# The kept scores of a top-k attention: one VectorE instruction per tile in place of two on GpSimd

## The reference

```python
scores = jnp.einsum('bhqd,bhkd->bhqk', Q, K) / np.sqrt(d)
k_keep = int(s * (1.0 - SPARSITY))                 # 25 of 256
vals, idx = jax.lax.top_k(scores, k_keep)
sparse = jnp.zeros((n, s), scores.dtype).at[rows, idx].set(vals)   # the rest is 0
attn = jax.nn.softmax(sparse, axis=-1)
out = jnp.einsum('bhqk,bhkd->bhqd', attn, V)
```

## Time and profile before

| what | value |
|---|---|
| three runs | 6017.2, 6035.1, 6035.79 us; median 6035.1 |
| the profiled execution, its own time | 6033.22 us |
| its span, first to last instruction | 6031.4 us |
| busy: PE, DVE, ACT, POOL | 5402.1, 4518.6, 3706.0, 2307.4 us |
| L1044, 4096 replaces, of these x1024 with m_last | mean 423 to 424 ns |
| granted TensorE clock, mean over the span | 0.934 |

### The profile page before, as it was taken

How to read it: one execution, slowest core, us unless ns; L and a number is a source line. 1 busy time by engine, 2 the same in 40 slices (tenths; PEclk the granted TensorE clock), 3 DMA queues, 4 the chain that set the end, 5 groups by cost and what they waited for, 6 DMA issues and landing times. The chain is left out here.

```text
span 6031.4 us, 113615 instructions
## 1 busy us (share of the span) xinstructions
PE 5402.1 (90%) x39450; PEld 3816.4 (63%) x39450; DVE 4518.6 (75%) x16189; ACT 3706.0 (61%) x9249; POOL 2307.4 (38%) x4100
## 2 busy tenths in 40 slices
PE   7899999899898999899998898989999899999987
PEld 4666666666666666566666666666666666666654
DVE  2477887777887777787777887777887777887774
ACT  3466676666676666666665666656666666676542
POOL 0233443334443334443333443334443334443341
PEclk7799999999999999999999999999999999998876
DMA  2000000000000000000000000000000000000000
GB/s 88 4 5 7 8 8 6 7 8 5 8 7 10 5 8 5 9 8 8 5 8 7 7 8 8 5 7 6 8 8 6 7 8 6 7 7 8 3 5 6
DMA packets 29387, 53.44 MB, mean 9 GB/s; under 512 B 8145, under 2 KB 9810, under 8 KB 27986
## 3 DMA queue, kind: packets, MB, share of 16 engines
q1 hardware_dynamic: 28770, 45.73, 2.5%
HBM read 37.33 MB, written 8.39 MB: 8 GB/s over the span
## 5 line engine op out<-in xcount | busy, mean ns | idle before, releaser
L1044 DVE MATCH_REPLACE8 wk<-m,wk 128x256 f32<-128x256 f32 x2048 | 835.9, 423 | 0.0
L1065 POOL TENSOR_SCALAR mx<-m 128x2 f32<-128x2 f32 x512 | 114.3, 223 | 1761.2 <-DVE wk L1044 1755.9
L479 DVE TENSOR_REDUCE m_nm<-bankM 128x2 f32<-128x512 f32 x1024 | 656.4, 692 | 168.6 <-PE bankM L469 166.4
L1040 DVE MAX8 m<-wk 128x8 f32<-128x256 f32 x2048 | 772.0, 425 | 0.0
L1074 POOL TENSOR_TENSOR t_pr<-wk,sc 128x256 f32<-128x256 f32 x1024 | 738.1, 741 | 3.8 <-issue 1.4
L1077 POOL TENSOR_TENSOR t_pr<-t_pr,sc 128x256 f32<-128x256 f32 x1024 | 728.4, 732 | 0.0
L810 ACT ACTIVATE xk_area<-bankH,xb 64x256 f32<-64x256 f32 x1024 | 479.8, 469 | 296.3 <-PE bankH L712 278.1
L1001 ACT ACTIVATE t_pr<-t_pr,t_nm 128x256 f32<-128x256 f32 x1024 | 475.9, 510 | 153.8 <-POOL t_pr L1077 141.5
L528 PE MATMUL bankM<-m_q,m_kT 32*128 32x512 f32 x2048 | 565.1, 631 | 0.0
L469 PE MATMUL bankM<-m_kT,m_q 32*128 32x256 f32 x4096 | 535.6, 399 | 10.3 <-DVE m_nm L479 8.9
L570 PE MATMUL bankT<-ident,t_pr 128*128 128x128 f32 x2048 | 342.9, 292 | 120.1 <-ACT t_pr L1001 117.7
(11 more groups left out here) (223 smaller groups left out, 11926.7 us busy)
## 6 DMA issues: line engine op xcount, KB each, us to landing
xin<-x_in SPq DMA_DIRECT2D x32, 256.0 KB, 2.6
ctxA<-ctx_in SPq DMA_DIRECT2D x32, 256.0 KB, 2.6
ctxB<-ctx_in SPq DMA_DIRECT2D x32, 256.0 KB, 2.8
out<-x SPq DMA_DIRECT2D x32, 256.0 KB, 2.0
w<-w_w SPq DMA_DIRECT2D x2, 1024.0 KB
xwq<-w_xwq SPq DMA_DIRECT2D x1, 1024.0 KB
xwk<-w_xwk SPq DMA_DIRECT2D x1, 1024.0 KB
xwv<-w_xwv SPq DMA_DIRECT2D x1, 1024.0 KB
```

What stands on the lines that cost most here:

```text
L479: nc.vector.tensor_reduce(b["nm"][:, i % 2, 2 * (i // 2) + x, :], banks[u % 4][:].rearrange("p (j s) -> p j s", j=2), AX.X, ALU.max, negat ...
L1040: link.inc(nc.vector.max(top, src[:, t, :]))
L1044: m = nc.vector.match_replace(out=wk[:, k, t, :], in_to_replace=take, in_values=src[:, t, :], imm_value=-BIG)
```

## The change

The two GpSimd instructions and their semaphore `sp_tk` go. VectorE makes the kept scores with one SCALAR_TENSOR_TENSOR per tile, (wk equals -2^64) times sc, right behind the head's last replace, and now waits itself for the transposes of head u-2. The exponential loses its scale. The buffer, the shift and all that TensorE does stay.

```diff
-        taken = sp_ = bufT["pr"]
+        sp_ = bufT["pr"]
...
                     nc.scalar.activation(b["pr"][:, u % 2, t, :], sp_[:, u % 2, t, :], ACT.Exp,
-                                         bias=b["nm"][:, u, t:t + 1], scale=-1.0 / BIG).then_inc(g["spa_ex"], 1)
+                                         bias=b["nm"][:, u, t:t + 1]).then_inc(g["spa_ex"], 1)
...
                 if u >= 2:
-                    dve.wait_ge(*at(g["sp_tk"], NT * (u - 1)))
                     dve.wait_ge(*at(g["sp_nm"], u - 1))
...
                     src = wk[:, k]
+                if u >= 2:
+                    dve.wait_ge(*at(g["spa_tr"], u - 1))
+                for t in range(NT):
+                    dve.wait_ge(*at(g["sp_top"], NT * u + t + 1))
+                    nc.vector.scalar_tensor_tensor(sp_[:, k, t, :], wk[:, k, t, :], -BIG, sc[:, u % 3, t, :], ALU.is_equal, ALU.mult).then_inc(g["sp_mul"], 1)
...
                 nc.gpsimd.tensor_copy(b["nm"][:, u, :], mx0[:, u, :]).then_inc(g["spa_nm"], 1)
-                yield
-                if u >= 2:
-                    pool.wait_ge(*at(g["spa_tr"], u - 1))
-                for t in range(NT):
-                    pool.wait_ge(*at(g["sp_top"], NT * u + t + 1))
-                    nc.gpsimd.tensor_tensor(taken[:, u % 2, t, :], wk[:, u % 2, t, :], sc[:, u % 3, t, :], ALU.subtract).then_inc(g["sp_tk"], 1)
-                for t in range(NT):
-                    pool.wait_ge(*at(g["sp_tk"], NT * u + t + 1))
-                    nc.gpsimd.tensor_tensor(sp_[:, u % 2, t, :], taken[:, u % 2, t, :], sc[:, u % 3, t, :], ALU.mult).then_inc(g["sp_mul"], 1)
```

```diff
     "pool": runs("""
-        c2 t h t2 c h2 t h t6 c t2 m t9 h2 t m t2 m h t h t3 h c t c t2 c t2 h t2 h t h t4 m t3 h c h t3 m t6 h2 t c2 t3 h2 t3 h t3 c t6 h
```

More of the change, by code:

```diff
@@ L79 @@
     "pe": runs("""
[L80 to L83, removed]
@@ new lines @@
+        c2 t c m h c h2 m2 t c h t h2 t m c m h c h2 t m2 h t m t h m t m h m c m h t h2 m h2 m t m2 t m2 t m2 h m h m t m t h t h2 m t m2 h3 t
+        h t h4 m h2 m2 h c h t m t m h t m t c2 t h3 c h2 t c h3 t2 h2 t h2 c t h t h t c h t c3 t h c t h t2 h2 c t c h4 c2 t h t c t c h c t
+        c2 h t2 h2 t h c2 t h3 t c2 t c h t h c h t h c2 h c t h t h c t c t h t h t c2 h c t h2 t h8 c h c t c t c t c t c t c2 t3 c t2 c t2 c
+        t2 c t c t c t2 c2 t c5 t c t2 c3 t c2 t c t2 c t c2 t4 c3 t3 c t5 c32"""),
@@ L99 @@
-        t6 h t3 h t3 h t h t8 h3 c5 t c t20 c t12 h t9 c2 t c t8 c t2 c7"""),
+        c2 t c h t2 h2 t h m t8 c m t2 m h t8 h t2 h t2 h c3 h t3 h t h2 m t4 h2 t c t h t2 c2 h t h t h t8 h t4 h c t2 h t2 h t2 h t4 h t2 h t2
+        h t h t5 h3 c5 t c t15 c t14 c3 t6 c7"""),
 }
@@ new lines @@
+        h c m h2 t c h t c t c h2 c t m h3 t h t2 c h2 m c m2 t h m2 t h m h t m h t m h m h m h t m h m t m t m t m5 t c m2 h t m h t m3 t m h
+        m2 h t m h t m t m h4 t h4 t h c h3 c t2 h t c t c2 m t c2 h2 c h2 t h c2 h t h2 c h t h c t h c t h c h c t c h t c h c2 t c h c t c h2
+        c2 t h c3 t h3 c t h c t h c h t h c h2 t h m t c t c h2 m2 t m h m2 h2 m t m h t h m t m h2 m2 t h t m t m t m2 t m4 h m2 t m t h m3 t
+        m h m2 h t m h t m t m h6 t h2 t h"""),
+    "act": runs("""
+        h2 c h t c h c h t h c t2 h t2 c h t5 h t h2 t h3 m t h2 t2 h t h2 t h t h2 t c2 h2 c t2 h2 t c2 h t h t2 c h2 t c2 t h2 t h2 c t c2 h t
+        h3 t c3 h4 t c h t h2 c t h3 c t c h t c h2 t h3 t h t c t h4 t h t3 h m t h2 t h3 t c h t h t h3 m4 t4 h2 t2 h t h t h t h2 t4 m t m t
+        m2 t m2 t m t c m2 t4 m2 t h m3 h t3 m2 t m2 h t h t m t h t m h t h2 c h c t h t h t c t3 h t3 c h t h t h7 t3 h2 t2 h3 t2 h t h2 c t
+        h2 t c2 h t h c2 t h2 t c t c t m t h2 t c h4 t c3 h4 t2 c3 h2 t h2 c t3 h t c h5 c2 h t c h t h4 t3 h c h5 t4 h t h m h t h c h3 t m t2
+        h m h m t m t h3 t2 h t2 h3 t3 h2 t5 m t m t m t2 m4 t2 m2 t2 m2 t h m3 t h t2 m2 t m h m t h m t2 h t m h t h c h2 t h c h2 c t h t c
+        t4 h c h t4 h t h2 t h3 t h t h3 t m t h t h t h2 t c2 h t h t h2 c t c2 t h t c h t h2 t c2 t h2 t h2 c t c t c h4 t c3 h4 t2 c h c h2
+        t h3 c t c h t c h t h4 t c h t2 h4 t h t3 h m t h2 t h3 t c t h2 t h2 m4 t3 h t h2 t h t h t h t h t h t4 m t m2 t c m2 t m2 t2 m2 t4
+        m2 h t m3 h t3 m2 t m2 t h2 t m t h t m h t h2 t h c h2 t h c t c t2 h t2 c h t3 h t h6 t3 h t h4 t3 h t h c t h3 c2 t h t h c2 t h2 t3
+        c m c t h2 t c h4 t c3 h4 t c t c2 h2 t h2 c t4 c h6 c2 h t c h t h4 t h t2 c h5 t4 h t h m t c h4 t h t2 m h2 m2 t m t h t h3 t h t2 h2
+        t h t h t6 m t m t2 m t m4 t2 m2 t2 m2 t h m3 h t3 m h m t m t m h m t2 h t m h t h"""),
@@ L136 @@
+        t2 h t h c2 t h c t5 h2 t2 m t2 h2 t2 c h t4 c t2 h t m t h c h t2 h t2 c t6 h t2 h m h t2 m t2 h c t c t h t h c t3 h2 t m t c t2 h2 m
+        t6 h c2 t2 h t h t h t4 c t2 h t4 h t2 m h t2 m h t h t c3 t2 h t2 h2 t h t3 m t2 h2 t2 h t4"""),
 }
@@ L159 @@
               mla_m3=1, mla_m3p=1, mla_nm=16, mla_on=2, mla_onT=1, mla_ont=1, mla_ot=2, mla_ott=1, mla_pv=8, mla_q=1, mla_qT=2, mla_rd=2,
-              mla_s=16, mla_sp=4, mla_st=16, mla_v=1, mla_va=1, mla_x=1, mla_y=1, sp_mul=32, sp_nm=16, sp_sc=16, sp_tk=32, sp_top=32,
+              mla_s=16, mla_sp=4, mla_st=16, mla_v=1, mla_va=1, mla_x=1, mla_y=1, sp_mul=32, sp_nm=16, sp_sc=16, sp_top=32,
               sp_xb=1, spa_ex=32, spa_k=1, spa_kT=2, spa_nm=16, spa_on=2, spa_onT=1, spa_ont=1, spa_ot=8, spa_ott=1, spa_pt=16, spa_pv=8,
```

82 lines of the change are left out of this document (33 added, 49 removed).

## The result

The changed kernel takes 1.0495 times as long as the one before (95% interval 1.0455 to 1.0534), 4.95% or about 299 us more. The profiled execution took 6334.2 us with a span of 6332.4, another 6318.5; two further executions were much slower, 6477.4 us at a granted clock of 0.799 and 20205.0 us, and are left out, so the ratio rests on two executions of the changed kernel. The forecast was 6175 us with a range up to 6300: the sign was right, the size about half of what was measured, and the time lies outside the range.

What follows compares the result with a forecast made beforehand. VectorE's unbroken row up to L907, for which TensorE waits at L768, was taken as the bound. Per lap 8.1 - 2.4 - 0.65 = +5.0 us; 28 laps +141, others +2, on 6033.2 gave 6175 us, range 6060 to 6300.

Steps and rivals of the forecast that it cites:

- The price of the instruction: New VectorE pair behind each head's last replace: 0.79 us a head, taken from L898, making 8.1 us a lap.
- rival 3: Much slower: GpSimd locks out the new VectorE instruction nearly every time, +15.2 us a lap, 6458 us; chance 0.07.
- the wait for `spa_tr`: New pair's first instruction waits for TensorE's transposes of the head before last; priced at nothing, over 30 us meaning wrongly priced.
- the forecast's 840: GpSimd's busy time was to fall from 2307 to some 840 us once its subtractions and products go.
- The bound: For the 80-odd us ahead of L907 VectorE runs without pause; time added there moves L768 and all behind it.
- a forecast of 5.0: Growth of a loop lap: 8.1 added, less 2.4 from quieter GpSimd, less 0.65 idle, +5.0 us.
- 10.25 heads: Heads per lap, of 16, whose new pair lies in VectorE's full stretch ahead of L907 and so costs time.
- a longer low clock: Longer wait at L768 may lengthen TensorE's 1.2 GHz stretch behind it, 1.7 us a lap; upper bound only.
- Time added outside falls into idle time: VectorE work outside its full stretch, five or six of a lap's 16 heads, costs nothing, since VectorE waits for TensorE there.
- The wait at L768: TensorE's wait for VectorE's L907 in stream h was to rise from 4.0 to some 9 us every loop lap.
- a wait under 5 us: Sign at L768: a wait this short would mean VectorE's stretch had cover that the forecast didn't see.
- The relief: VectorE's L902, L907 and lnM_xn run faster without GpSimd's pair beside them: 2.4 us a lap, 67 us in all.

Runs made afterwards that it cites:

- the kernel without the step: Changed kernel without VectorE's new pair, ScalarE taking the exponential of all scores, so the selection is missing from the output: 5973.0 us, 0.9922 of the kernel before.
- the pair with fillers: Two kernels with one more filler everywhere: kernel before plus two MAX8 per head on VectorE, GpSimd's pair kept, 6294.7 us; changed kernel, 6239.6 us.
- the MAX8 stand-in: Kernel before, GpSimd's two instructions kept, with two unused MAX8 per head added on VectorE, old fillers: 6291.7 us, 1.0438 of the kernel before.

## Why the prediction was half right

- **The price of the instruction** was near, and somewhat high: one takes 417 ns, and the pair moves the next start by 0.67 us (2850.81 to 2851.48 in the rows below) where the sum used 0.79. L1053 itself is never locked out beside GpSimd, so rival 3 falls, and so does any cost of the wait for `spa_tr` (1.2 us over the span). What collides is held on GpSimd's side, its copy L1072. That is 198 of the 262 us by which GpSimd's 1102.7 us exceed the forecast's 840.
- **The bound** held in its place: a lap grows only ahead of L907. Its size is not confirmed. With the clock repaired at five places a lap grows by 5.3 us for a forecast of 5.0, but 266 fillers and 2.9 us of low time (worth 1.4 us) are in the 5.3, and with one more filler everywhere on both sides it grows by 4.4, 2.0 without the low clock. Inside the 5.0, too, two misses cancel: 10.25 heads at 0.67 us are 6.9 us and not 8.1, and the stretch from L898 to L907's end shrank by 1.0 us (3.55 to 2.54) and lnM_xn gave 0.3, 1.3 together and not 2.4. The agreement is partly luck.
- **The step that failed** is the clock, "a longer low clock" priced at nothing in the sum and at up to 1.7 us a lap in the upper bound. It measured 9.3 us. The price was taken from the one pause at L768, as if only a longer pause there could lower the clock. In fact other hand-overs that hang on VectorE's row moved with it, directly (m_nm, lnH_xn) or over ScalarE (xp); several small ones became pauses of 1 to 3 us, and low stretches of some 14 to 24 us followed. Behind them TensorE at half speed was the bound, and VectorE stood idle, 3.5 us of the 84 on average for 2.0 before, in the very stretch that the forecast took as VectorE's alone.
- **"Time added outside falls into idle time"** held for VectorE's row up to head 5 and failed for the lap, for the same reason: heads 0 to 5 were absorbed and cost 110 us all the same. In the changed kernel VectorE idles 40.8 us a lap for 40.0: the idle time that was to take five or six heads was not used up.
- **The wait at L768** was to rise to 9 us; it fell to 3.5. The forecast had read a wait under 5 us as a sign of cover in the stretch; it was none, since the lap grew by twice the forecast. TensorE comes later to L768, since it has been delayed ahead of it. Even with fillers at five places it is 127.2 us in 30 times, the 4.2 us of before. A wait tells how far two rows are apart, not how late both are.
- **The relief** was 47 us by the kernel without the step, 24 to 64 by the pair with fillers, for 67 forecast. L902, L907 and lnM_xn gave back 20.2 + 26.6 + 10.0 = 56.8 us. L898 took 13.5 of it: GpSimd, free earlier, now adds stream h's residual (L939) beside it. VectorE and then GpSimd in the changed kernel's timeline:

```profile
2850.81 0.75 DVE L1053 SCALAR_TENSOR_TENSOR t_pr<-wk,sc 128x256 f32<-128x256 f32 x2
...
2851.48 1.88 DVE L898 SCALAR_TENSOR_TENSOR xv<-xv,scol,lower 128x256 f32<-128x256 f32 x2
2853.28 0.47 DVE L902 SCALAR_TENSOR_TENSOR xv<-xv,scol 128x256 f32<-128x256 f32 x1
```

```profile
2851.56 1.50 POOL L939 TENSOR_TENSOR xa<-xa,lnH_xn 128x512 f32<-128x512 f32 x1
```

L898 takes 1.88 us for two where the earlier trace rows had 0.90; L902, behind it, is rid of GpSimd. The Trainium skill, SBUF — State Buffer, section Who interferes with whom, says that such a pair of instructions lock each other out, the later one waiting for the earlier. The trace agrees: the longest L898 takes 1497 ns, the length of L939 (1.50 us), and 14 of the 64 take as long; each of these starts 0.30 us behind an L939 and ends 0.28 us behind its end; L1072, which starts behind the first L1053, takes 732 ns at the median where it took 184. The forecast looked at whom the old pair disturbed and not at what would move into the gap.

What stays open: why the fall lasts some 3 us in one place and 24 in another was not settled, only that a short pause stands ahead of the long ones and that filler matmuls at it take them away. Nor were the 161 us that the kernel with fillers at five places still loses split by experiment into waiting, the fillers' own time and what is left of the low clock, nor is the longer L1072 priced.

## What to carry to other kernels

When work is added to the engine that TensorE takes its inputs from, look at every hand-over between them and not only at the longest wait: a pause of 1 to 3 us in TensorE's row can leave it at half speed for 20 us, and that can cost as much as the work itself. So compare the granted clock and TensorE's busy time at the same count of matmuls first; here idle time explained 1.1 of 10.4 us a lap. If such a change is made all the same, place filler matmuls again from the new trace: 266 of them gave back 138 us, where 1530 spread evenly gave back 88.

## What the hardware showed that I had not expected

- TensorE's clock stood at 0.50 for 20 us while TensorE was busy for 3.3 to 4.0 us of every 4. What one fall costs, 10 us, is several times the pause of 2 us ahead of it.
- Two kernels with nearly the same work differ by 34 us against the order of their work (the MAX8 stand-in and the changed kernel), because the pauses fall in other places. A part of a change can't be priced from such a pair unless the low time is equal.
- The same added work cost 18 to 19 us per head in three places of the lap, once by waiting and twice mostly by the clock.
- Two VectorE instructions that keep their own length can still stretch a GpSimd instruction beside them from 184 ns to 732.
